# One-hot chunks used where they are made: the first pick of a four-stage graph network on one Trainium2 core

## The reference

```python
# network 0, four layers
m = x[src] @ W.T + b;  s = x[dst] @ W.T + b
logit = m @ Wa[:, :HIDDEN].T + s @ Wa[:, HIDDEN:].T
a = jnp.exp(jax.nn.leaky_relu(logit, negative_slope=0.2))
n = jax.ops.segment_sum(a, dst, num_segments=n_nodes)
h = jax.nn.relu(x / jnp.where(n == 0.0, 1.0, n))
x = _rmsnorm(h + x, nw, nb)
y = jax.nn.relu(x @ hW.T + hb)
x = _rmsnorm(x + y, hnw, hnb)
# network 1
e = el[src] + er[dst] + rel_w[etype]          # then a softmax over each dst, and a weighted sum of nfeat[src]
```

## Time and profile before

| | us |
|---|---|
| median of 3 runs (5943.95 to 5957.6) | 5945.24 |
| the profiled execution | 5958.42 |
| its span, first to last instruction | 5956.6 |
| PE busy (108221 matmuls) | 3969.0 |
| DVE busy | 3499.9 |
| ACT busy | 2094.0 |
| POOL busy | 736.3 |
| mean granted clock of TensorE | 0.84 |

### The profile page before, as it was taken

One profiled execution on the slowest core, in us unless ns is written; L12 is line 12 of the kernel. 1 busy time (PEld: TensorE's weight loads), 2 busy tenths in 40 slices (PEclk: granted clock), 3 DMA queues, 4 the chain that ended last, 5 costly groups with the idle time before them and its releaser, 6 DMA issues.

```text
span 5956.6 us, 236270 instructions
## 1 busy us (share of the span) xinstructions
PE 3969.0 (67%) x108221; PEld 3202.8 (54%) x108221; DVE 3499.9 (59%) x4015; ACT 2094.0 (35%) x2443; POOL 736.3 (12%) x758
## 2 busy tenths in 40 slices
PE   0015514804724813818888888887999988999997
PEld 0005513803723812806666666666988976666665
DVE  4532711731571741847676666666535539999997
ACT  4100000011001010007676676664635624555453
POOL 0033263072133033040000000000000000000000
PEclk9996755955865955959999999998989978999998
DMA  6722400520420501511111111114525510000000
GB/s 173 235 64 68 123 17 8 165 63 4 141 74 1 172 6 32 169 49 52 52 57 51 52 58 51 52 49 135 178 100 168 178 65 10 10 11 11 10 11 16
DMA packets 229352, 437.54 MB, mean 73 GB/s; under 512 B 115490, under 2 KB 139940, under 8 KB 228628
## 3 DMA queue, kind: packets, MB, share of 16 engines
q1 hardware_dynamic: 204784, 416.14, 22.1%
q0 software_dynamic: 23904, 10.76, 0.9%
HBM read 317.98 MB, written 112.84 MB: 72 GB/s over the span
## 4 chain that ended last, share of the span: by engine, by line
PE 62%; issue 15%; DVE 12%; ACT 3%; DMA 2%; another core or an unknown queue 2%; POOL 2%; SPq 2%; DVEq 0%; ACTq 0%; POOLq 0%
PE psum L987 16%; PE psum L959 12%; PE psum L836 12%; PE psum L1017 10%; PE psum L947 3%; PE psum L867 2%; PE psum L823 2%; DMA space<-digit_rows 2%; ACT space L709 1%; DVE space L1461 1%; PE psum L869 1%; DVE space L1143 1%; PE psum L1026 1%; PE psum L816 1%
## 5 line engine op out<-in xcount | busy, mean ns | idle before, releaser
L714 ACT COPY space<-psum 128x784 f32<-128x784 f32 x1184 | 966.2, 816 | 631.1 <-PE psum L959 629.0
L959 PE MATMUL psum<-space 64*128 64x49 bf16 x56832 | 990.4, 185 | 181.5 <-issue 152.3
L959 PEld LDWEIGHTS psum<-space 64*128 64x128 bf16 x56832 | 855.7, 95 | 391.2 <-issue 282.9
L987 PE MATMUL psum<-space,X 128*64 128x256 f32 x7252 | 1041.1, 398 | 13.6 <-issue 11.1
L836 PE MATMUL psum<-table,space 128*128 128x56 bf16 x24300 | 701.9, 189 | 347.8 <-issue 333.8
L836 PEld LDWEIGHTS psum<-table,space 128*128 128x128 fp8e4 x24300 | 671.3, 96 | 378.2 <-issue 367.2
L1268 DVE TENSOR_REDUCE space<-psum 128x1512 f32 x300 | 520.0, 1733 | 531.0 <-remote 379.0
L1461 DVE TENSOR_TENSOR space<-space 128x2352 bf16<-128x2352 bf16 x592 | 815.0, 1377 | 0.0
L1457 DVE TENSOR_TENSOR space<-space,V 128x2048 bf16<-128x2048 bf16 x592 | 721.5, 1219 | 0.0
L1017 PE MATMUL psum<-space 128*128 128x192 bf16 x7252 | 628.4, 247 | 23.9 <-DVE space L1536 23.9
L709 ACT CAST space<-psum 128x784 uint8<-128x784 f32 x592 | 482.9, 816 | 400.7 <-PE psum L947 398.1
(11 more groups left out here) (277 smaller groups left out, 2785.8 us busy)
## 6 DMA issues: line engine op xcount, KB each, us to landing
space<-onehots SPq DMA_DIRECT2D x300, 432.0 KB
space<-adj_d SPq DMA_DIRECT2D x148, 784.0 KB, 4.3
adj_d<-space SPq DMA_DIRECT2D x74, 784.0 KB, 3.6
onehots<-space SPq DMA_DIRECT2D x60, 432.0 KB, 2.9
space<-digit_rows SPq DMA_DIRECT2D x60, 378.0 KB
space<-cw_d SPq DMA_DIRECT2D x74, 160.0 KB, 3.3
cw_d<-space SPq DMA_DIRECT2D x4, 1184.0 KB
heads_d<-spread,heads_at POOLq DMA_INDIRECT x280
```

The costliest lines, as they stand in the source:

```text
L714: nc.scalar.copy(A[:, h, :, b * P:(b + 1) * P].rearrange("p a (w s) -> p w a s", w=2)[:, :, :, c:c + UC], psum[:, 2 + 2 * (k % 2):4 + 2 * ...
L959: mm = nc.tensor.matmul(psum[:, 2 + 2 * (k % 2) + w, c * NB:(c + 1) * NB], ohlo[lo:hi, ring, col // 2, :, col % 2], ohw[lo:hi, ring, r, co ...
L987: mm = nc.tensor.matmul(pb[6][half:half + F, 0:2 * P], X[:, a, :], A[:, 1 - h, a, :], start=(a < 2), stop=(a >= NB - 2))
```

## The change

It does these things.

1. `first_pick` makes and uses the chunks in one loop. For each chunk n DVE does `columns(n)` and then `pick_of` chunk n - 1; PE multiplies chunk n straight out of `ohb`. The chunks are still stored for the later picks; the 60 loads of the first pick from DRAM are gone. `bcast` and `ohb` become rings of four (`bcast` moves to the arena).
2. For that, the transpose of x, the scalars and the table of layer one move ahead of the loop. DVE's first lines are put in another order: base rows and x first, digits, then the codes, the weights' copies and the zeroing of `heads_d`.
3. The loop is cut in three phases: chunks 4 to 19, 20 to 39, 40 to 59. After the first DVE does `first_rows` (the tile numbers, which release POOL's 49 gathers), after the second `row_bounds` (49 compares, row pointers, heads). POOL's `scatter_heads(0)` waits for `heads_found`, which comes out of `row_bounds`.
4. The relation weights go to layer four, behind its second scan (`relations`); the edge types are loaded in layer three instead of at the start.
5. The memsets of `xT` go to POOL, the four DMAs of the row pointers from SP to ACT's queue, the Sign results to their own place `signs`, three stores of codes and two small DMAs of SP ahead of its loop.

```diff
+PHASES = [(1, 5), (5, 10), (10, NCH // OR)]
@@ SP
-            for h in range(2):
+            for h in range(OR):
                 digits_in(h, slice(h, h + 1))
...
+            with sp.Fori(1, NCH // OR) as i:
+                for h in range(OR):
+                    sp.wait_ge(oh_made, i * OR + (h + 1 - OR))
                     sp.sem_inc(sp_ok, 1)
+                    sp.dma_start(onehots[bass.ds(i * OR + (h - OR), 1)].rearrange("a p e -> (a p) e"), ohb[:, h, :]).then_inc(oh_saved[h], 16)
+                    digits_in(h, bass.ds(i * OR + h, 1))
...
             for k in range(LAYERS):
-                pick_loads(k)
+                if k:
+                    pick_loads(k)
@@ POOL
             def scatter_heads(n):
 
                 pool.wait_ge(spread_ready, n + 1)
+                pool.wait_ge(heads_found, 1)
@@ PE
+            def first_pick():
+
+                pe.wait_ge(table_ready, 1)
+                for h in range(OR):
+                    pe.wait_ge(oh_made, h + 1)
+                    if h >= 2:
+                        pe.wait_ge(pick_read, h - 1)
+                    chunk_from(ohb, h)
+                for phase, (lo, hi) in enumerate(PHASES):
+                    with pe.Fori(lo, hi) as i:
+                        for h in range(OR):
+                            pe.wait_ge(oh_made, i * OR + (h + 1))
+                            pe.wait_ge(pick_read, i * OR + (h - 1))
+                            pe.sem_inc(pe_ok, 1)
+                            chunk_from(ohb, h)
+                    if phase == 1:
+                        pe.wait_ge(rp_ready, 2)
...
@@ DVE
+                for phase, (lo, hi) in enumerate(PHASES):
+                    with dve.Fori(lo, hi) as i:
+                        for h in range(OR):
+                            dve.wait_ge(bc_loaded[h], i * 48 + 48)
+                            dve.wait_ge(oh_saved[h], i * 16)
+                            columns(h)
+                            dve.wait_ge(pick_psum, i * OR + h)
+                            pick_of(bass.ds(i * (OR * CH) + (h - 1) * CH, CH), (h - 1) % 2)
+                    if phase == 0:
+                        first_rows()
+                    if phase == 1:
+                        row_bounds()
...
+                if k == 3:
+                    relations()
```

More of the change, by code:

```diff
@@ L372, in _ @@
                 sp.wait_ge(padded, 16 * 10)
-                for tile, pad in ((srcFi, src_pad), (dstFi, dst_pad), (etyF, ety_pad)):
+                for tile, pad in ((srcFi, src_pad), (dstFi, dst_pad)):
                     sp.dma_start(tile, pad.rearrange("(p t) -> p t", t=TF)).then_inc(loaded, 16)
@@ L825, in scalars, with chunk_from @@
                 mm.then_inc(pq_psum, 1)
+            def chunk_from(rows, h):
+                for b in range(NBK):
+                    for t in range(PB):
+                        c = (b * PB + t) * P
+                        for r in range(3):
+                            mm = nc.tensor.matmul(pb[(h % 2) * NBK + b][:, t * HI:(t + 1) * HI], rows[:, h, c:c + P].bitcast(FP8),
+                                                  table[:, r, :], start=(r == 0), stop=(r == 2))
+                mm.then_inc(pick_psum, 1)
@@ L827, in pick @@
             def pick(k):
                 pe.wait_ge(table_ready, k + 1)
-                def chunk(h):
-                    for b in range(NBK):
-                        for t in range(PB):
-                            c = (b * PB + t) * P
-                            for r in range(3):
-                                mm = nc.tensor.matmul(pb[(h % 2) * NBK + b][:, t * HI:(t + 1) * HI], ohr[:, h, c:c + P].bitcast(FP8),
-                                                      table[:, r, :], start=(r == 0), stop=(r == 2))
-                    mm.then_inc(pick_psum, 1)
@@ L1144, in columns @@
                                         ALU.mult).then_inc(oh_made, 1)
-            for h in range(2):
-                dve.wait_ge(bc_loaded[h], 48)
-                columns(h)
-            with dve.Fori(1, NCH // 2) as i:
-                for h in range(2):
-                    dve.wait_ge(bc_loaded[h], i * 48 + 48)
-                    dve.wait_ge(oh_saved[h], i * 16)
-                    columns(h)
-            dve.wait_ge(counted, NB)
-            link(nc.vector.tensor_scalar(small[:, 1, :], small[:, 0, :], 0.5, TT / 2.0 - 1.0, ALU.mult, ALU.add))
@@ L1157, in _ @@
-            link(nc.vector.tensor_scalar(small[:, 1, :], small[:, 1, :], 0.0, None, ALU.max))
-            dve.wait_ge(padded, 160)
-            nc.vector.tensor_copy(starts[:, :], small[:, 1, :]).then_inc(rp_ready, 1)
-            dve.wait_ge(drows, 16 * NB)
-            for j in range(NB):
-                link(nc.vector.tensor_scalar(junk[:, 0:P], dstrows[:, j * P:(j + 1) * P], node_id[:, j:j + 1], None, ALU.is_lt,
-                                             ALU.add, accum_out=small[:, 0, j:j + 1]))
@@ L1338, in slots @@
                 dve.wait_ge(enc_stored, 48)
+                for h in range(OR):
+                    dve.wait_ge(oh_saved[h], 16 * (NCH // OR))
                 dve.wait_ge(consts, 4)
@@ L1369, in slots, with relations @@
                 link(nc.vector.tensor_copy(slot_base[:, :], slot_dst[0:1, :]))
+            def relations():
+                dve.wait_ge(ety_loaded, 16)
+                for e in range(NTYPES):
+                    link(nc.vector.tensor_scalar(rel_sum if e == 0 else rel_of, etyI, float(e), relw[:, e:e + 1], ALU.is_equal, ALU.mult))
+                    if 0 < e < NTYPES - 1:
+                        link(nc.vector.tensor_tensor(rel_sum, rel_sum, rel_of, ALU.add))
+                nc.vector.tensor_tensor(rel_sum, rel_sum, rel_of, ALU.add).then_inc(rel_w_ready, 1)
             for k in range(LAYERS):
-                pick(k)
+                if k == 0:
+                    first_pick()
+                else:
+                    pick(k)
                 spread_heads(2 * k, k)
```

272 lines of the change are left out of this document (148 added, 124 removed).

## The result

The changed kernel took **5652.45 us** (median of four runs, 5648.93 to 5670.12), the kernel before 5944.59 beside it (four runs, 5940.28 to 5957.6): ratio 0.951, 95% interval 0.949 to 0.954. That is 292 us less where 176 were forecast. The time lies 116.6 us under the forecast, 15.6 under the low end of the range, and 22 under rival one. The sign was right; the size and the mechanism that carried it were not.

A forecast was written before the change was run, and what follows sets the result against it. It saw start-up stretches without overlap and PE's completions late beside POOL's DMA trains. Pick's end 88.7 + 244 + 31.4 + 131.5 = 495.6 against 675.6, 180.0 less, layer four +4: span 5780.6, median 5769 us, range 5668 to 5805.

The forecast's parts named there:

- rival one: First pick: the loop doesn't trickle beside POOL's trains; 5674 us (0.13) or 5638 if compares don't hold POOL (0.04); chance 0.17.
- POOL's two trains: First pick, 49 gathers and 56 scatters beside the loop: late PE completions cost 63.9 + 67.6, together 131.5 us; other end nothing.
- 60 chunks, with filling: First pick's loop: 4.0 us a chunk between 3.75 and 4.4, 240 us, and 4 to fill and drain.
- layer four: Relation weights moved behind its second scan: DVE's instructions delay POOL's gather train; +4 us, between 0 and 10.
- Rival two: First pick: chunks slip through before each train bites, or a milder trickle; 5700 to 5735 us, chance 0.09.
- Rival three: First pick: compare, chunk and reduction one after another, PE at lower clock, 8.1 us a chunk; 6015 us, chance 0.03.
- (a): Sign in the new trace: layer one's table near 89 us, the first pick's last reduction near 496.
- (b): Sign in the first pick: reductions 3.8 to 4.4 us apart where POOL is silent.
- (c): Sign in each POOL train: one gap of 60 us or more between reductions, matmuls 2.8 us apart; none means rival one.
- (d): Sign in the first pick: `row_bounds` takes 31 us.
- (e): Sign in layer four: relations end 3 us after the first part of its gather.
- The two rules weighed: Skill rules: PE holds 2048 instructions, so a loop would escape a fetch trickle; a two-port tensor_scalar locks GpSimd out.

The follow-up runs named there:

- the loop from the first chunk on: Changed kernel with PE's first four chunks of picks two to five inside its loop instead of straight-line code; 5665.9 us (one run).
- small compares: Changed kernel whose compares in the first pick's third phase cover 128 of 3456 columns, so DVE hardly holds POOL; 5710.2 us (one run).
- T1: Follow-up theory, not a run: straight-line matmuls trickle beside POOL's indirect DMAs, a loop does not.
- T2: Follow-up theory, not a run: PE is held where POOL issues an indirect DMA each 1.24 us; the compare slows POOL and that frees PE.
- the relations kernel: Changed kernel with DVE's fifteen relation-weight instructions moved from layer four to the start of the fourth pick; 5220.8 us, kernel before 5399.
- second group: Runs of three pause lengths between POOL's scatters and of the relation weights moved to pick four; kernel before 5399 us there.
- fourth group: Runs of half the rows per scatter, of two kernels with memsets between scatters and chunk gathers, and of the changed kernel; kernel before 5939 us.
- the kernel with half the rows: Changed kernel with each scatter of picks two to five writing 56 rows instead of 112; 5660.4 us (one run).
- with pauses: Changed kernel with two small POOL memsets between scatters of picks two to five; 5204.0 us where the kernel before took 5399.
- at most two in flight: Changed kernel with at most two unlanded POOL scatters allowed in picks two to five; 5624.4 us, 0.946 of the kernel before.

## Why the prediction was wrong

**The step that failed** is "I take the upper end", in the part on POOL's two trains. The ends were 0 and 131.5 us and the reason for the upper one was that late completions hurt a loop as much as straight-line code. That is true (the loop from the first chunk on; the small compares), but it is no answer to whether POOL would run at the pace at which completions are late. The rows for this were on the table: the add that made a DMA take 3.63 us, and a compare in each chunk. I used them for rival one alone, as a cost ("if the compare holds POOL"), and asked T1's question of them. The two facts should have been put together: a pace of 2 us is not the pace of the earlier trace rows. What the runs showed in its place: beside the compares POOL issued a DMA per 1.97 us, PE ran 1470 and 1605 matmuls in 80 us, and the two trains cost 33.3 us, their own length beyond the loop; with small compares and 1.24 us a DMA the standstill came back with 72.76 us.

By terms, in the profiled executions:

| term | forecast | measured |
|---|---|---|
| table ready | 88.7 | 90.0 |
| 60 chunks, with filling | 244 | 231 |
| row pointers | 31.4 | 31.3 (252.33 to 283.67) |
| the two trains | 131.5 | 33.3 |
| first scan starts | 495.6 | 385.1 |
| layer four | +4 | +10.4 |

The trains are 98 of the 110 us in the pick. The chunks give 13: 3.57 us while POOL is silent and some 3.95 beside it, where I had 4.0 throughout with 3.75 as the floor. Layer four gives 6.4 back. In spans the change is 129.0 us under the forecast (5651.6 against 5780.6), so 24.9 are in neither; 12.4 of these come from the profiled execution of the kernel before, which lay 13.2 over its median where that of the kernel after lay 0.9 over, and 12.5 of the 116.6 remain. They lie after the pick, where the change adds only the load of the edge types and layer four's work, and are of the size by which executions of one program differ: from the scan of pick three to that of pick four two profiles of the kernel before took 411.9 and 398.5 us, two of the kernel after 402.7 and 412.3.

**Rival one** had the mechanism, T2's half of it: two DMAs per chunk, and 36 us of waiting for the DMAs left over, 14 for the gather and 22 for the scatters and the load of the heads (measured 12.2 and 21.1). With the loop as measured it gives 5674 - 13 - 3 + 1 + 6 = 5665, less the 12.5 that no term has 5653. It had 0.13 and should have been the likeliest. Rival two (5700 to 5735) didn't come: nothing between, since the pace in both phases was on the free side. Rival three (one after another) didn't either: PE was granted 0.93 to 0.97 of its clock in the loop, so not its lower level, and the reductions of the chunk before covered it.

**The list of what would show it**: (a) the table at 90 yes, the last reduction at 381 and not near 496; (b) 3.57, below the stated 3.8 to 4.4; (c) no gap of 60 us, DMAs in pairs: as the prediction has it, that is rival one; (d) 31 us, yes; (e) the relations ended 8 us before the first part of the gather and not 3 after, because the part itself came 10 us later.

**Layer four**: the mechanism (DVE's adds hold POOL's train) was right and in its rows, the size was not: fifteen instructions cost 10.4 us, the upper end, and the relations kernel shows the other side: with them gone from layer four the wait is 19.79 us again.

**The two rules weighed.** The loop trickled when POOL ran at full pace: 85 matmuls in 65 us, and PE's queue fetched no instructions in that time. The rule of the Trainium skill, Runtime: NRT & Kernel Launch, section Instruction fetch mechanics, by which the loop would escape, therefore says nothing on this hold; it led me to test the form of the code and not the pace. The compare of 2.01 us made POOL's DMA 2.40 us in place of 0.94. The Trainium skill, SBUF — State Buffer, section Who interferes with whom, has a two-port tensor_scalar lock GpSimd out; the trace agrees in kind if the compare is one, which no row says, and one DMA still gets through at 0.94 between two compares.

**What stays open.** In four groups (the first measurement among them) the kernel before took 5939 to 5949 us, in one 5399, where PE was not held at all. The records give the same number of the chip for the second and the fourth group, of which one has the hold and the other not; whether that is one chip in two conditions isn't told by them. So the cause beneath is not found, only its dependence on the number of DMAs in a time.

The traces do show one more difference between the two conditions. Each scatter raises its semaphore by 16 as it lands, and the profile keeps records of that. In the train of pick two the kernel after has 135 such records for 55 scatters (880 raises), the kernel with half the rows 132, the relations kernel in the second group 755. So the profile can give a time to landing there and not here (gathers, kernel after and relations kernel):

```profile
gath<-scans_d,ends POOLq DMA_INDIRECT x196
gath<-scans_d,ends POOLq DMA_INDIRECT x196, 2.4
```

Where PE is held, most of these records are missing. Every execution here has a span and a clock of its own, so none is known to have run unrecorded. That the hold lies in the recording, and that the 320 us of the memsets and part of the change's gain go with it, is a rival that no run here tests.

How much the change itself gains without the hold is not measured either: the kernel after didn't run in that group. Its variants did: from 5399 to 5204 with pauses and 5221 with the relations moved, so some 180 to 195 us instead of 292. By these, 97 to 114 us of the gain seen here, over a third, would be a standstill avoided (an estimate); the one in the first pick was 75.67 us long.

## What to carry to other kernels

Where an engine "waits for nothing" beside a train of small DMAs, measure its progress against the pace of the train, and price a move of that train by the pace that it will have in its new place, not by the one in the trace. An operation that holds an engine can be a gain: here a compare that took POOL from 1.24 to 1.97 us a DMA was worth some 44 to 58 us in one phase, and two idle memsets per DMA took off 320 more, both under the condition that PE is held. Before a result of this kind is trusted, look at the kernel before in each group of runs.

## What the runs showed that I had not expected

- 56 indirect DMAs at 1.24 us each let PE run 1.6 matmuls a us (111 in 68.1 us), at 1.86 us each 25.7; halving the rows of each changed nothing (104 in 66 us).
- The hold needs a few DMAs to set in and lets PE go some us after the last: with at most two in flight PE ran 637 matmuls in 30 us beside 15 scatters, then 35 in 37 beside 30.
- The same program ran without any hold in one group of runs (2489 matmuls in 69 us beside the full train), 549 us faster as a whole for the kernel before.
- Where PE was held the profile kept 135 of 880 records of the scatters' landings in a train, where it wasn't some 750 of as many.
- Neighbouring DVE operations overlapped by about 0.1 us each: a compare of 2.01 and a reduction of 1.72 repeated every 3.57 us.
